# Output projections of a decoder kernel: the last unit's products behind four heads, Wo heads 8 to 11 head by head, Wo loads ahead of kept rows, and the first expert's split between the norms

## The reference, cut to what matters

```python
x = _layernorm(x + _L0_attn_ref(x, ...))    # self0:  2 x 512 tokens, 16 heads of 128, rope, causal
x = _layernorm(x + _L0_xattn_ref(x, ctx))   # cross0: 1024 context tokens, rms norm of q and k
x = _layernorm(x + _L0_ffn_ref(x, ...))     # ffn0:   4 experts, token n goes to expert n % 4
x = _layernorm(x + _L1_attn_ref(x, ...))    # self1:  causal
x = _layernorm(x + _L1_xattn_ref(x, ctx))   # cross1: 8 k/v heads
x = _layernorm(x + _L1_ffn_ref(x, ...))     # ffn1:   weights and rows rounded to fp8 with scales
```

## Time and profile before

| | |
|---|---|
| three runs | 2650.91, 2655.49, 2658.30 us; median 2655.49 |
| the profiled execution | 2651.95 us, its span 2650.2 us |
| busy share of the span | TensorE 92%, VectorE 70%, ScalarE 60%, GpSimd 27% |
| TensorE's granted clock, mean | 0.969 |
| output projections on TensorE | self0 442 to 536, cross0 1227 to 1339, self1 1812 to 1901, cross1 2419 to 2507 us |
| the experts of ffn0 | from 1353.8 us |
| the final FFN (ffn1) | from 2512.1 us |
| issue to landing, median | Wo load (256 KB, self) 2.9 us, Wdown block (704 KB) 4.9 us, an expert's gate and up (2048 KB) 8.3 us |
| GpSimd busy between 494.43 and 535.80 us | 24.39 of 41.37 us |

### The profile page before, as it was taken

The page is one execution under the profiler, slowest core; times in us unless marked ns, Lnnn a source line. Parts: engine busy times, 40 slices in busy tenths (PEclk is TensorE's granted clock), DMA queues, the critical chain, the costliest instruction groups (busy, mean ns, idle before and its releaser), DMA issues. The chain is left out here.

```text
span 2650.2 us, 57668 instructions
## 1 busy us (share of the span) xinstructions
PE 2442.6 (92%) x21584; PEld 1567.2 (59%) x21584; DVE 1849.5 (70%) x3371; ACT 1590.4 (60%) x2718; POOL 720.4 (27%) x671
## 2 busy tenths in 40 slices
PE   7999998989999999999678999999999999999964
PEld 4565555446666666665345666665466666665432
DVE  5777777557777777775556666668487888884597
ACT  5767775158777878884133555664177777774242
POOL 5666665601110011012233222225200000012211
PEclk9999999999999999999888999999999999999987
DMA  3333335225666666666340444446178777776400
GB/s 95 88 77 82 89 75 132 90 57 106 118 115 118 106 110 116 117 110 136 107 167 1 93 93 93 95 91 148 19 140 147 143 146 149 148 147 129 106 1 32
DMA packets 769428, 273.83 MB, mean 103 GB/s; under 512 B 737904, under 2 KB 740720, under 8 KB 767600
## 3 DMA queue, kind: packets, MB, share of 16 engines
q1 hardware_dynamic: 767504, 265.82, 48.0%
q0 software_dynamic: 1760, 5.77, 0.7%
HBM read 84.55 MB, written 6.44 MB: 34 GB/s over the span
## 5 line engine op out<-in xcount | busy, mean ns | idle before, releaser
L875 ACT ACTIVATE phl<-p,ri 128x1024 bf16<-128x1024 f32 (+4 forms) x512 | 437.3, 854 | 413.3 <-DVE ri L1184 387.4
L1194 DVE SCALAR_TENSOR_TENSOR phl<-p,ri,phl 128x1024 bf16<-128x1024 f32 (+4 forms) x512 | 511.7, 999 | 103.3 <-issue 75.1
L886 ACT ACTIVATE p<-p,nb 128x1024 f32<-128x1024 f32 (+4 forms) x512 | 435.8, 851 | 54.2 <-DVE nb L1177 39.8
L1255 PE MATMUL ps<-wo_lo,v_hi 128*128 128x128 bf16 x2496 | 439.3, 219 | 0.0
L1254 PE MATMUL ps<-wo_hi,v_hi 128*128 128x128 bf16 x2240 | 395.8, 219 | 23.2 <-DMA wo_hi<-phl 16.0
L1256 PE MATMUL ps<-wo_hi,v_lo 128*128 128x128 bf16 x2240 | 395.6, 219 | 0.0
L1254 PE MATMUL ps<-k_hi,q_hi 128*128 128x512 bf16 (+3 forms) x768 | 272.7, 355 | 22.3 <-DVE nb L1175 20.1
L1255 PE MATMUL ps<-k_lo,q_hi 128*128 128x512 bf16 (+3 forms) x768 | 272.2, 354 | 0.0
L1256 PE MATMUL ps<-k_hi,q_lo 128*128 128x512 bf16 (+3 forms) x768 | 271.9, 354 | 0.0
L1255 PEld LDWEIGHTS ps<-wo_lo,v_hi 128*128 128x128 bf16 x2496 | 244.9, 98 | 33.2 <-issue 0.3
L1254 PEld LDWEIGHTS ps<-wo_hi,v_hi 128*128 128x128 bf16 x2240 | 219.3, 98 | 68.7 <-DMA wo_hi<-phl 28.1
(11 more groups left out here) (197 smaller groups left out, 6140.0 us busy)
## 6 DMA issues: line engine op xcount, KB each, us to landing
raw_kv<-in_wkvself SPq DMA_DIRECT2D x32, 512.0 KB, 3.7
raw_q<-in_wqself SPq DMA_DIRECT2D x32, 256.0 KB, 2.6
raw_q<-in_woself SPq DMA_DIRECT2D x32, 256.0 KB, 2.9
raw_q<-in_wqcross SPq DMA_DIRECT2D x32, 256.0 KB, 2.9
raw_q<-in_wocross SPq DMA_DIRECT2D x32, 256.0 KB, 3.0
wo_hi<-phl SPq DMA_TRANSPOSE x384, 3.2
wo_lo<-phl SPq DMA_TRANSPOSE x384, 3.1
raw_kv<-in_wkvcross SPq DMA_DIRECT2D x24, 256.0 KB, 3.2
```

Source lines behind the costliest of these rows:

```text
L875: nc.scalar.activation(m["ph"](qt, w), m["p"][:, qt % 2, 0:w], ACT.Copy, scale=ri[:, qt % 2:qt % 2 + 1]).then_inc(p_norm, 1)
L886: nc.scalar.activation(prob, prob, ACT.Exp, scale=1.0 if L.rms else -1.0, bias=nb[:, qt % 2:qt % 2 + 1], accum_out=rs[:, qt % 2:qt % 2 + 1 ...
L1194: nc.vector.scalar_tensor_tensor(out=m["pl"](qt, w), in0=m["p"][:, qt % 2, 0:w], scalar=ri[:, qt % 2:qt % 2 + 1], in1=m["ph"](qt, w), op0= ...
L1255: nc.tensor.matmul(o, l(0), r(1), start=False, stop=False)
```

## The change

1. In all four attention layers, the last unit's `weigh` calls move ahead on TensorE: behind head 3 of tiles 0 to 3 instead of behind head 7.
2. Heads 8 to 11 are added to tiles 0 to 3 head by head, each behind its own wait for Wo, ahead of the wait for all heads. Tiles 0 to 3 then lack only heads 12 to 15.
3. `turn_x` calls follow a table: two tiles each behind tile 4 and tile 5, one each behind the later ones. (Before ffn1 the transposes stay where they were.)
4. In cross0 SyncE loads Wo 10 to 15 ahead of the stores and loads of Wdown blocks, and behind these loads the first expert's gate and up weights.
5. The first expert's split moves from ffn0's start into cross0's norms: ScalarE's copy behind `x_part` 1, GpSimd's subtract behind `inv_std(3)`, VectorE's at the end of step 5.

```diff
 # SyncE
-                        sp.dma_start(m["raw_gu"][e % 2], a["gu"][e]).then_inc(gu_in[e % 2], 16)
+                        if e:
+                            sp.dma_start(m["raw_gu"][e % 2], a["gu"][e]).then_inc(gu_in[e % 2], 16)
...
                 for h in range(10, H):
                     wo(h)
-                    if L.rms and h in (11, 12):
-                        keep(h)
-                        load_down(h + 2)
+                if L.rms:
+                    for k in (11, 12):
+                        keep(k)
+                        load_down(k + 2)
+                    sp.dma_start(mem[li + 1]["raw_gu"][0], a["gu"][0]).then_inc(gu_in[0], 16)
...
 # GpSimd
-                    gate_low(0)
...
                     inv_std(t)
...
+                    if L.rms and t == 3:
+                        f = mem[li + 1]
+                        pool.wait_ge(gu_hi, 1)
+                        pool.wait_ge(y_mm, c["ln"] + 1)
+                        nc.gpsimd.tensor_tensor(f["gu"][1][:, 0, :, 0:FFN_I], f["raw_gu"][0][:, :, 0:FFN_I], f["gu"][0][:, 0, :, 0:FFN_I], ALU.subtract).then_inc(gate_lo, 1)
...
 # ScalarE
-                    gu_high(0)
...
                         x_part(li + 1, NT * (li + 1) + t, t, t)
+                        if L.rms and t == 1:
+                            f = mem[li + 1]
+                            act.wait_ge(q_ok, 15)
+                            act.wait_ge(o_mm, c["u"] + UNITS)
+                            act.wait_ge(q_kept[0], kept_count(15))
+                            act.wait_ge(gu_in[0], 16)
+                            nc.scalar.activation(f["gu"][0][:, 0, :, :], f["raw_gu"][0], ACT.Copy).then_inc(gu_hi, 1)
...
 # VectorE
-                    up_low(0)
...
+                    if L.rms and k == 5:
+                        f = mem[li + 1]
+                        dve.wait_ge(gu_hi, 1)
+                        dve.wait_ge(y_mm, c["ln"] + 1)
+                        nc.vector.tensor_tensor(f["gu"][1][:, 0, :, FFN_I:2 * FFN_I], f["raw_gu"][0][:, :, FFN_I:2 * FFN_I], f["gu"][0][:, 0, :, FFN_I:2 * FFN_I],
+                                                ALU.subtract).then_inc(up_lo, 1)
...
 # TensorE
                     for t in range(4):
                         project(t, h, h == 0, False)
-                for qt in range(QT - LAG, QT):
-                    weigh(UNITS - 1, None, qt)
+                    if h == 3:
+                        for qt in range(QT - LAG, QT):
+                            weigh(UNITS - 1, None, qt)
...
+                for h in range(8, 12):
+                    pe.wait_ge(w_split, c["split"] + H + h + 1)
+                    for t in range(4):
+                        project(t, h, False, False)
                 pe.wait_ge(w_split, c["split"] + 2 * H)
+                turns = {4: (0, 1), 5: (2, 3), 6: (4,), 7: (5,), 8: (6,), 9: (7,)}
                 for t in range(NT + 2):
                     if t < NT:
-                        for h in range(8, H):
+                        for h in range(12 if t < 4 else 8, H):
                             last = project(t, h, False, h == H - 1)
...
-                    elif t >= 2:
-                        pe.wait_ge(ln_x, c["ln"] + t - 1)
-                        turn_x(t - 2, t - 2)
+                    else:
+                        for k in turns.get(t, ()):
+                            pe.wait_ge(ln_x, c["ln"] + k + 1)
+                            turn_x(k, k)
```

## The result

| | us |
|---|---|
| before, median of 4 | 2656.52 (2650.91 to 2658.3) |
| changed, median of 4 | 2617.64 (2614.38 to 2619.85) |
| ratio, 95% interval | 0.9858, 0.9846 to 0.9871 |
| profiled execution of the changed kernel: time, span | 2614.38, 2612.6 |

Forecast were 2619 us and a range of 2610 to 2631. To see whether the terms held too, the span is cut at TensorE's own marks: the first product of each output projection, and the first product of the layer behind it.

The account below looks back on a forecast made before the run. TensorE's own work plus its waits bounds each projection, chiefly 20.91 us on cross0's Wo split. Terms -6.5 - 1.7 - 22.7 - 9.1 + 1.2 + 2.7 = -36.1 us give 2615.9 for the profiled execution, median 2619, range 2610 to 2631.

Parts of the forecast that it names:

- the norms: Cross0's norms around GpSimd's moved subtract: TensorE waits 1.1 us for norm 4 and 0.1 at tile 7, +1.2 us.
- Self0: Self0's output projection: loses TensorE's 3.7 us wait on the Wo split and a 2.8 us cold restart, -6.5 us.
- the restart: TensorE coming back at a lower clock after idling in a projection: costs 2.8 us in self0, 1.8 us in cross0.
- Self1: Self1's output projection: TensorE's 1.71 us wait on the Wo split goes, with no cold restart counted, -1.7 us.
- Cross0: Cross0's output projection: the whole 20.9 us wait on the Wo split goes with its 1.8 us cold start, -22.7 us.
- rival 4: Cross0's wait does not go whole, splits hanging on something besides SyncE's order; 10 us more gives 2629; 0.07 with another rival.
- The quantising: VectorE's rounding of Wdown rows in cross0 ends at 1289 and costs nothing; beyond 1292 would be wrong.
- Rival 2: Cross0's quantising ends later than 1289; with the rest of Rival 1 the time is 2623 to 2629; together 0.17.
- The first expert: Start of the first FFN expert: its copy and subtract are done before the tail, so TensorE starts at x_lo, -9.1 us.
- Rival 1: Cross0's norm 3 falls into GpSimd's 6.16 us subtract: +4.6 us, 2624; chance 0.17 together with Rival 2.
- Cross1: Cross1's projection: tiles 0 to 3 come later, VectorE passes lateness on to the final FFN, +2.7 us, bounds 0 and 3.4.
- Rival 5: Kernel slower than before: ScalarE's moved first-expert copy waits for a late store of the last kept row; chance 0.02.

Follow-up runs that it names:

- both best kernels: Changed kernel with cross1's projection in the old order and the second expert's split two Silus earlier, without and with SyncE's old order: 2608.84 and 2609.5 us.
- the two kernels that undid a part: Changed kernel with the last unit's products behind eight heads again, 2625.34 us; changed kernel with all sixteen heads tile by tile again, 2629.61 us.

## Why the prediction was right, point by point

The spans differ by 37.6 us where the sum had 36.1. No large errors cancel in it: self0 gave 0.4 us less than forecast, self1 0.4 more, the norms 1.2 more, cross1 0.6 more, and the untouched stretches together came out 0.3 us longer.

- **Self0, -6.5, measured -6.1.** The reasoning held: the wait went by the heads done ahead of it, not by the earlier products (with heads 8 to 11 alone self0 gains 7.2, with the products alone nothing). What was missed is that the last unit's products, now behind four heads, can come before their own transposed weights. TensorE waits 0.45 us there in self0 of the changed kernel, in other runs up to 2.8; I had counted that margin for cross0 only (there no run shows a wait). One reading was wrong without harm: of the two stretches that I said hold about 25 products, the one in self0 holds 13; the restart's 2.8 us were taken from VectorE's start and do not hang on it.

```profile
453.77 0.23 PE L1272 MATMUL ps<-wo_lo,v_hi 128*128 128x128 bf16 x1 [0.45 <-DMA wo_lo<-phl]
```

- **Self1, -1.7, measured -2.06.** The wait is gone, but the size isn't settled: by the same marks the stretch took 92.3 to 97.4 us in kernels without the wait. The traces show where part of it goes. In some kernels with the last unit's products behind four heads TensorE stands idle among them: 0.19 and 1.87 us in the kernel with cross1's old order, whose stretch is 94.85 us, and nowhere in the one with late products and SyncE's old order, whose stretch is 92.30. In both best kernels one such row names the transposed weights (0.49 and 0.66 us), but most of them name no releaser, so the cause stays open:

```profile
1786.86 0.22 PE L1273 MATMUL ps<-wo_hi,v_hi 128*128 128x128 bf16 x1 [1.87 <-issue]
```

- **Cross0, -22.7, measured -22.75, and its reason half wrong.** The two shares of four heads are there one by one, 10.9 and 10.4 us, and 1.4 us are left for the restart, where I had 1.8. The step that put the rest on SyncE's order ("Before, SyncE kept Wo 12 and 13 back for two stores") failed: with the old order the wait goes as well. The number for this stood in rival 4, that at the old pace the chain would end "just when TensorE asks". It does, 0.4 us ahead, and nothing is lost; I had both facts and credited the wrong one.
- **The quantising.** Counted from cross0's projection, which comes 6.77 us earlier, the last split is at 1264.2 (forecast 1262 to 1266) and the last rounding at 1292.5: later than my 1289 and than the 1292 that I had named as a sign of being wrong. Its price was still 0, by 1.0 us. Rival 2 was the real danger here, and the two kernels that undid a part ran into it, by 7.0 and 6.0 us.
- **The first expert, -9.1, measured -9.06** with the norms in it, where I had -9.1 + 1.2 = -7.9. ScalarE's copy and GpSimd's subtract began as forecast (1300.1 and 1303.8 on the old clock). Norm 4 was to cost 1.1 us: it waited 2.37 us for its rstd, ended at 1302.57, and TensorE came for it at 1303.87, so there was no wait. So the term that was wrong is the norms' +1.2: it measured 0, because its 6.16 us for GpSimd's subtract are 4.08 us away from VectorE's. That is all of the difference between -30.6 and -31.8 in the table. Rival 1 was priced too high for the same reason.
- **Cross1, +2.7, measured +2.09.** VectorE starts tile 0 where it was expected, and steps run back to back. I took 5.17 us a step, from a stretch with idle of its own; the timeline of VectorE shows 2448.68 for tile 3 and, four steps on, 2468.97, so 5.07 us a step, and more of the lateness is given back:

```profile
2448.68 0.68 DVE L1028 TENSOR_TENSOR xf<-ps,xf 128x512 f32<-128x512 f32 x1
...
2468.97 0.68 DVE L1028 TENSOR_TENSOR xf<-ps,xf 128x512 f32<-128x512 f32 x1
```

- **Rival 5** (slower, by a late store) didn't come about: ScalarE's copy at 1293.37 waited for nothing.

What stays open: why the experts' stretch varies by some 5 us where nothing in it is changed, beyond the clock of the first 5 us; and whether the last unit's products should stay behind eight heads in self0 and self1. The runs suggest it (three self0 stretches with late products are 92.3 to 93.2 us, eight with early products 92.8 to 95.3, in kernels that all have heads 8 to 11 ahead), but no kernel with that alone was run.

## What to carry to other kernels

When a wait is longer than one edit can cover, price each edit by itself against the same question of the waiting engine. Of three edits that all help, the last may buy nothing, and an order of loads often only moves slack between two chains, so write down both slacks. A duration read while two engines share a port is not the duration of the work alone: look for the same row without its neighbour before using it for a moved instruction. A copy that prepares a layer belongs as early as its load allows, since an idle TensorE costs the wait and then a restart at 1.2 GHz.

## What the runs showed of the hardware

- GpSimd's 128x2048 subtract took 4.06 to 4.08 us with no subtract of VectorE beside it and 6.17 us when VectorE's subtract of the same kind began 0.04 us ahead of it, and VectorE's took 2.29 us either way: the engine that came second paid all, 2.1 us. By the Trainium skill, page "SBUF — State Buffer", section "Who interferes with whom", whoever issues first has the shared port pair for the whole instruction and the other fully blocks; these rows agree, and the earlier trace rows show it the other way round. I had seen the rule at work on VectorE's 6.14 us only, and not that GpSimd's own 6.16 us held 2.1 us of it.
- The first expert starts at a granted clock of 0.50 (1.2 GHz) for its first 5 us although TensorE was idle for only 1.74, 0.64 and 1.42 us ahead of it, with short transposes between. Behind 10.47 us of idle, in the kernel before, its first 5 us look the same (0.53, 25 products). Shortening that idle bought the idle itself and nothing of the restart.

```profile
1353.77:1358.77 5.00, 5.00 (x25) 3.62 (x26) 2.04 (x1) 0.00 (x0) 0.00 (x0) 0.53 0.86 308
```

- With the second expert's copy early TensorE keeps its clock through the change of experts, and for a wait of 4.99 us that is gone the second expert's start comes 5.15 us earlier and its 49th product 7.3 us earlier. Most of the restart's price falls behind the first product, so a step from start to start does not show it.
